# A graph-attention gather loop: the softmax shift from the weights, the running maximum kept ahead of the slope, its parts as upper halves of words

## The chip, the cores and the metric

One core of a Trainium2 chip runs the whole program. The metric is the device time of one execution in microseconds; lower is better.

## What is computed

A GPS layer over 6250 nodes of 256 features and 100000 edges, then a mixture of six experts. `src` is the row (segment) of an edge, `dst` the node that it reads:

```python
# x: [6250, 256], src, dst: [100000]; xn = layernorm(x)
Wh = xn @ W + b
e = (Wh @ a[:256])[dst] + (Wh @ a[256:])[src] + a_b
e = where(e > 0, e, 0.2 * e)
m = segment_max(e, src)                   # one maximum per row
ex = exp(e - m[src])
h = relu(segment_sum(ex / segment_sum(ex, src)[src] * Wh[dst], src))
x = x + h + linear_attention_block(xn)    # with a feed-forward of 1024 and two norms
x = x + experts(layernorm(x))             # 6 experts, top 2
```

## The kernel before

The program is three blocks. The first (to about 754 us) normalises, projects Wh into a table in HBM, computes the linear attention and sorts the edges by rows into tiles of 128. The rows are taken in 50 blocks of 125. The second block (to about 2000 us) is the gather loop. The third is the expert stage.

A row of the table holds 256 values of Wh, the destination term f_dst (column D) and a 1.0 for the denominator: WROW = 258. GpSimd gathers one tile of 128 table rows per indirect DMA (line 1283) into a ring of 44 tiles; SP counts what has landed (`ready`, line 1273) and what has been used (`room`, line 1268).

The other engines work on groups of four tiles that belong to one block, 251 groups. Each engine has a queue written out by hand: `together` takes a list of (lag, stage) and issues, in slot s, each stage for group s - lag. Twenty slots are the body of a loop. In ten slots one pair of row blocks also passes the feed-forward (`feed`: 4 slots of hidden products, 4 of down products on TensorE, the sum and norm on VectorE at slots 0 and 2). One group passes:

- ScalarE fetches its row numbers (`own_rows`, L1459). VectorE adds the shift to the four destination terms of each partition (`shifted`, L1315) and writes for each tile a matrix with that term in the column of the edge's row, zero elsewhere (`mark`, L1322). TensorE turns the four (`turn`, L1565). The terms must be positive for this, which is what the shift is for: one minus the smallest destination term of all nodes, computed after the projection (L688 to L690, L1096, L798 to L802).
- Two slots later VectorE takes the maximum over the group (`group_peak`, L1332), adds the row term (`row_score`, L1338), applies the slope (`row_leaky`, L1343), takes the maximum with the running one (`new_max`, L1350), forms old less new (`old_less_new`, L1357) and keeps it (`keep_max`, L1364). ScalarE makes the turned matrix a 0/1 matrix (`spread`, L1445).
- Three slots after the marks ScalarE splits the new maximum into three bf16 parts (`own_high`, `own_mid`, `own_low`, L1470 to L1483), which stand beside three parts of the row term in `own_all`, computes the factor for old sums (`rescale`, L1489) and distances (`apart`, L1499); TensorE brings row term and maximum to the edges by a product with the 0/1 matrix (`fetch`, L1575).
- Four slots after, VectorE computes the edge's exponent (`score_sum`, `score_edge`, `score_leaky`, `score_less_max`, L1371 to L1388), ScalarE the weight of the last tile (`edge_exp`, L1506) and of the others (`weigh`, L1513), VectorE the last tile's matrix (`own_weight`, L1395).
- Five slots after, TensorE sums weighted rows (`total`, L1586, 8 products) and VectorE adds them to the block's sum (`gather_up`, L1406).

TensorE's queue in a slot is total, fetch, feed-forward products, turn. A helper computes the register address of anything that depends on the group's place or block (L1301, L1308).

## Time and profile before

| | us |
|---|---|
| runs shown | 2505.85, 2507.08, 2512.12; median 2507.08 |
| span of the profiled execution | 2505.8 |
| busy over the span: TensorE, VectorE, ScalarE, GpSimd | 2000.0, 1914.7, 1479.9, 1212.4 |
| gather loop: first gather to last start of line 1406 | 754.4 to 1979.7 |
| third block, 2000 to 2506: TensorE busy | 383.7 |

The profiled execution is 1.3 us under the median. Engines are named PE (TensorE), DVE (VectorE), ACT (ScalarE), POOL (GpSimd), SP; a q behind a name is its instruction queue, where register work stands. In a timeline each row is one instruction (or several merged, xN) with its start, its duration and, in brackets, the idle time of the engine before it and what ended it.

### The profile page before, as it was taken

What the parts mean: (1) busy time and instruction counts of PE and PEld (TensorE: products, weight loads), DVE (VectorE), ACT (ScalarE), POOL (GpSimd) and SP (SyncE); (2) the same over time, 40 slices, a digit from 0 to 9 for tenths busy, and PEclk for the clock granted to TensorE, in tenths of its full rate; (3) what the DMA queues carried; (4) which work ended last, traced back from release to release, by engine and by line L of the source; (5) the groups of instructions that cost most, each with busy time, mean ns of one, the idle gap of its engine ahead of it and who ended that gap; (6) DMA issues with size and microseconds to landing.
All of it is one profiled execution on the core that took longest, in us unless ns stands there. A gap on an engine that the chain in (4) does not pass through costs nothing. (4 is left out here: it accounts for less than half of the span.)

```text
span 2505.8 us, 55059 instructions
## 1 busy us (share of the span) xinstructions
PE 2000.0 (80%) x10267; PEld 1596.8 (64%) x10268; DVE 1914.7 (76%) x6441; ACT 1479.9 (59%) x4950; POOL 1212.4 (48%) x1141
## 2 busy tenths in 40 slices
PE   2888856688855898898888888988989665199997
PEld 1444435577744677677777767767767554188886
DVE  7877689999966898898898898898899763045553
ACT  3566457233304787778788778777878662033332
POOL 0000000011127777777777777777771067455554
PEclk9899967799967899999999989989999866599998
DMA  4200000011113444444444434344440355345553
GB/s 138 54 25 28 25 5 21 13 54 25 21 24 104 119 113 118 114 111 117 113 113 118 110 105 113 111 115 114 117 113 29 92 145 141 86 76 93 94 97 57
DMA packets 125788, 211.73 MB, mean 84 GB/s; under 512 B 35583, under 2 KB 78492, under 8 KB 125476
## 3 DMA queue, kind: packets, MB, share of 16 engines
q0 software_dynamic: 71952, 141.08, 23.7%
q1 hardware_dynamic: 48866, 60.24, 8.2%
q10 hardware_dynamic: 4658, 7.46, 1.0%
q14 instruction: 263, 2.15, 0.3%
q8 instruction: 49, 0.80, 0.1%
HBM read 152.62 MB, written 49.70 MB: 81 GB/s over the span
## 5 line engine op out<-in xcount | busy, mean ns | idle before, releaser
L1283 POOL DMA_INDIRECT area<-wh_table,area x860 | 866.5, 1008 | 284.6 <-issue 257.0
L1586 PE MATMUL bank<-area 128*126 x2008 | 532.7, 412 | 29.4 <-ACT area L1513 20.5
L1586 PEld LDWEIGHTS bank<-area 128*126 128x126 f32 x2008 | 386.2, 203 | 105.0 <-issue 49.5
L1322 DVE TENSOR_SCALAR area<-iota_row,area 128x126 f32<-128x126 f32 x1004 | 343.4, 357 | 0.4 <-issue 0.2
L1499 ACT ACTIVATE area<-iota_row,area 128x126 f32<-128x126 f32 x753 | 269.9, 390 | 0.0
L2077 POOL DMA_INDIRECT out_dram<-area x108 | 169.5, 1569 | 159.3 <-DVE area L2136 142.6
L1513 ACT ACTIVATE area<-area 128x126 f32<-128x126 f32 x753 | 242.4, 385 | 0.0
L515 POOL IOTA acc_mem<- 50x860 f32 x1 | 0.8, 846 | 457.5 <-DVE area L784 457.5
L1606 PE MATMUL bank<-area 128*128 128x250 f32 x800 | 211.4, 410 | 0.0
L1617 PE MATMUL bank<-area 128*125 128x256 f32 x800 | 197.1, 389 | 0.0
L1332 DVE TENSOR_REDUCE area<-bank 125x1 f32<-125x512 f32 x251 | 171.0, 681 | 26.6 <-issue 13.6
L1565 PE MATMUL bank<-ident,area 128*126 128x128 f32 x1004 | 159.5, 283 | 26.7 <-DVE area L1322 26.7
L1445 ACT ACTIVATE area<-bank 125x512 bf16<-125x512 f32 x251 | 144.7, 576 | 59.7 <-DVE area L1332 59.6
L1606 PEld LDWEIGHTS bank<-area 128*128 128x128 f32 x800 | 156.5, 206 | 17.0 <-ACT area L1519 0.2
L1575 PEld LDWEIGHTS bank<-own_all,area 125*128 125x128 bf16 x1004 | 55.0, 99 | 173.7 <-issue 156.5
L1565 PEld LDWEIGHTS bank<-ident,area 128*126 128x126 f32 x1004 | 125.5, 144 | 51.9 <-DVE area L1322 17.4
L2136 DVE SCALAR_TENSOR_TENSOR area<-bank,area 128x256 f32<-128x256 f32 x108 | 47.5, 479 | 145.0 <-DMA out_dram<-area 85.8
L520 POOL DMA_INDIRECT sorted_slots<-area x28 | 46.0, 1641 | 229.3 <-DVE area L855 216.5
L1617 PEld LDWEIGHTS bank<-area 128*125 128x125 f32 x800 | 142.0, 187 | 16.9
L1776 POOL DMA_INDIRECT moe_rows<-area x100 | 120.8, 1208 | 64.7 <-ACT area L1927 35.1
L1575 PE MATMUL bank<-own_all,area 125*128 x1004 | 63.3, 168 | 104.5 <-ACT own_all L1483 84.6
L1406 DVE SCALAR_TENSOR_TENSOR acc_mem<-acc_mem,area,bank 125x258 f32 x251 | 121.2, 483 | 32.2 <-PE bank L1586 24.2
(387 smaller groups left out, 4468.4 us busy)
## 6 DMA issues: line engine op xcount, KB each, us to landing
area<-moe_rows SPq DMA_DIRECT2D x54, 264.0 KB, 2.8
area<-wh_table,area POOLq DMA_INDIRECT x860
area<-area SPq DMA_DIRECT2D x19, 387.0 KB
wh_table<-area SPq DMA_DIRECT2D x50, 126.0 KB
xn<-in_x_dram SPq DMA_DIRECT2D x25, 250.0 KB
x_rows<-area SPq DMA_DIRECT2D x25, 250.0 KB
area<-x_rows ACTq DMA_DIRECT2D x24, 250.0 KB
area<-in_L_ffn_expert_w_dram SPq DMA_DIRECT2D x3, 1536.0 KB, 12.2
```

The costliest lines, as they stand in the source:

```text
L1283: g.indirect_dma_start(out=gath[:, (i + GT) % RS, :], out_offset=None, in_=table, in_offset=bass.IndirectOffsetOnAxis(ap=idx_tab[:, i:i + ...
L1322: ins = V.tensor_scalar(xm[:, b, t, :], iota_row[:, :], rowl[:, j % 10, t:t + 1], fdc[:, b, t:t + 1], ALU.is_equal, ALU.mult)
L1332: V.tensor_reduce(gmax[0:R, b:b + 1], bank[XT[j % 2]][0:R, :], AX.X, ALU.max).then_inc(d_m, 1)
L1406: V.scalar_tensor_tensor(row, row, alpha[0:R, j % 5:j % 5 + 1], bank[US][0:R, 0:WROW], ALU.mult, ALU.add).then_inc(d_acc, 1)
L1445: A.activation(hot[0:R, b, :], bank[XT[j % 2]][0:R, :], ACT.Sign).then_inc(a_hot, 1)
L1499: last = A.activation(dist[:, b, t, :], iota_row[:, :], ACT.Abs, bias=rowl[:, j % 10, t:t + 1], scale=-1.0)
L1513: last = A.activation(sm[:, b, t, :], dist[:, b, t, :], ACT.Exp, bias=e3[:, b, t:t + 1], scale=-1.0e12)
L1565: last = T.transpose(bank[XT[j % 2]][0:RW, t * L:(t + 1) * L], xm[:, b, t, :], ident[:, :])
L1586: last = T.matmul(bank[US][0:RW, 0:WROW], sm[:, b, t, :], gath[:, bass.ds(place + t, 1), :].rearrange("p a w -> p (a w)"), start=(t == 0), ...
L1606: last = T.matmul(bank[HB[p % 2]][:, i * CH:(i + 1) * CH], w_1[:, k, f * 128:(f + 1) * 128], x1T[:, k, :], start=(k == 0), stop=(k == 1))
L1617: last = T.matmul(bank[AB][0:R, r * D:(r + 1) * D], hT[:, f, r * R:(r + 1) * R], w_2[:, f, :], start=(f == 0), stop=(f == 7))
L2077: g.indirect_dma_start(out=out, out_offset=bass.IndirectOffsetOnAxis(ap=rowi[:, j % RB6, s, MW - 2:MW - 1], axis=0), in_=yo[:, j % 3, s, : ...
```

## The change

- A table row has 259 values (TW): column D holds f_dst plus the shift, column D + 1 the 1.0, column D + 2 plain f_dst. `mark` reads column D itself; `shifted` and its buffer are gone. All columns come out of one product with a wider weight matrix, and one addition of a wider bias.
- The shift is 8 times the squared length of the weight vector of f_dst, plus 9, from the weights alone, before the projection (two small products on TensorE at the start). The reduction over nodes and its product are gone.
- The running value `peak` is the maximum of the scores before the slope; the slope is applied to it afterwards. Five VectorE steps on the maximum become two (`row_peak`, `row_leaky`). The old maximum is read from `own_all` by `rescale`, which now computes exp(old - new) itself and stands ahead of the write of the new one.
- `own_all` has fp32 words. A part of a value is the upper half (bf16) of its word, seen through `own_bits`; the next word is the value less that half. On ScalarE the splitting is three steps instead of four.
- The orders of VectorE's and ScalarE's queues change as in the two lists below.
- SP's and VectorE's register values for some waits are bounded by one more register step each.

```diff
+TW = D + 3
...
-        own_all = sb("own_all", [R, NT, 6], BF16)
+        own_all = sb("own_all", [R, NT, 6])
+        own_bits = own_all[:, :, :].rearrange("p b k -> p (b k)").bitcast(BF16).rearrange("p (b k h) -> p b k h", k=6, h=2)[:, :, :, 1]
...
-                    V.tensor_copy(frd[:, t, :], bank[2 + t % 2][0:R, D:D + 2])
-                    V.tensor_tensor(whs[0:R, t % 4, 0:D + 1], bank[2 + t % 2][0:R, 0:D + 1], bias_g[0:R, :], ALU.add).then_inc(p_row, 1)
+                    V.tensor_copy(frd[:, t:t + 1], bank[2 + t % 2][0:R, TW:TW + 1])
+                    V.tensor_tensor(whs[0:R, t % 4, :], bank[2 + t % 2][0:R, 0:TW], bias_g[0:R, :], ALU.add).then_inc(p_row, 1)
...
                 def weights():
...
+                    V.memset(w_a[:, :, D + 1:D + 2], 0.0)
...
-                        for i, vec in enumerate((a_dst, a_src)):
+                        for col, vec in ((D, a_dst), (TW, a_src)):
...
-                                                        accum_out=w_a[:, k, D + i:D + i + 1]))
+                                                        accum_out=w_a[:, k, col:col + 1]))
+                    V.tensor_tensor(wsq, w_a[:, :, D], w_a[:, :, D], ALU.mult).then_inc(w_ready, 1)
+                    V.tensor_copy(w_a[:, :, D + 2], w_a[:, :, D])
...
-                    V.tensor_copy(cdst, bias_g[:, D:D + 1])
+                    V.tensor_copy(bias_g[:, D + 2:D + 3], bias_g[:, D:D + 1])
...
+                    dve.wait_ge(sq_sum, 1)
+                    step(V.tensor_scalar(shift[:, :], bank[2][:, 0:1], 8.0, 9.0, ALU.mult, ALU.add))
+                    step(V.tensor_tensor(bias_g[:, D:D + 1], bias_g[:, D:D + 1], shift[:, :], ALU.add))
...
-                V.tensor_reduce(neg1[0:R, :], frd[:, :, 0], AX.X, ALU.min).then_inc(sh_diag, 1)
-                dve.wait_ge(sh_diag, 2)
-                V.tensor_scalar(fdiag[0:R, 0:R], ident[0:R, 0:R], neg1[0:R, :], None, ALU.mult).then_inc(sh_diag, 1)
...
-                dve.wait_ge(gmap_done, 1)
-                step(V.tensor_reduce(scol, bank[KV][:, 0:R], AX.X, ALU.min))
...
-                step(V.tensor_scalar(scol, scol, cdst, None, ALU.add))
-                step(V.tensor_scalar(shift[:, :], scol, -1.0, 1.0, ALU.mult, ALU.add))
-                step(V.tensor_scalar(fr[:, :], frd[:, :, 1], csrc[0:R, :], None, ALU.add))
-                step(V.tensor_copy(own_all[:, :, 0], fr[:, :]))
-                step(V.tensor_tensor(fr_c[:, :], fr[:, :], own_all[:, :, 0], ALU.subtract))
-                step(V.tensor_copy(own_all[:, :, 1], fr_c[:, :]))
-                step(V.tensor_tensor(own_all[:, :, 2], fr_c[:, :], own_all[:, :, 1], ALU.subtract))
-                V.tensor_scalar(fr_c[:, :], fr[:, :], shift[0:R, :], None, ALU.subtract).then_inc(shift_done, 1)
+                step(V.tensor_scalar(own_all[:, :, 0], frd, csrc[0:R, :], None, ALU.add))
+                step(V.tensor_tensor(own_all[:, :, 1], own_all[:, :, 0], own_bits[:, :, 0], ALU.subtract))
+                V.tensor_tensor(own_all[:, :, 2], own_all[:, :, 1], own_bits[:, :, 1], ALU.subtract)
+                V.tensor_scalar(fr_c[:, :], own_all[:, :, 0], shift[0:R, :], None, ALU.subtract)
...
+                for k in range(2):
+                    last = T.matmul(bank[2][:, 0:1], ones[:, :], wsq[:, k:k + 1], start=(k == 0), stop=(k == 1))
+                last.then_inc(sq_sum, 1)
...
-        gath = take(RS + GT - 1, WROW)
+        gath = take(RS + GT - 1, TW)
...
-        mrun = take(NT)
+        peak = take(NT)
...
+                used = sp.alloc_register("used")
...
-                        sp.reg_load(uses[f % 2], group_tab[32:33, f - RING:f - RING + 1])
+                        sp.reg_load(used, group_tab[32:33, f - RING:f - RING + 1])
+                        sp.reg_alu(uses[f % 2], used, 1, ALU.max)
...
-                V.memset(mrun[0:R, :], -1.0e30)
+                V.memset(peak[0:R, :], -1.0e30)
+                V.memset(own_all[:, :, 3:4], -1.0e30).then_inc(acc_zero, 1)
...
-                def dst_terms(j):
...
-                def shifted(s, j):
...
+                def fetched(j, col):
+                    return gath[:, bass.ds(dve.snap(places[j % 10], min_val=0, max_val=RS - 1), GT), col]
...
                     def stage(s, j):
...
-                        dve.wait_ge(d_x, at(s, 2, 1))
-                        ins = V.tensor_scalar(xm[:, b, t, :], iota_row[:, :], rowl[:, j % 10, t:t + 1], fdc[:, b, t:t + 1],
+                        if t == 0:
+                            dve.wait_ge(a_row, at(s, 1, 1))
+                            wait(dve, p_xt, at(s, 1, -1))
+                        ins = V.tensor_scalar(xm[:, b, t, :], iota_row[:, :], rowl[:, j % 10, t:t + 1], fetched(j, D)[:, t:t + 1],
...
-                def row_score(s, j):
+                def row_peak(s, j):
...
-                    dve.wait_ge(d_m, at(s, 6, 1))
-                    V.tensor_tensor(gt[0:R, b:b + 1], gmax[0:R, b:b + 1], fr_c[:, bass.ds(r, 1)], ALU.add).then_inc(d_m, 1)
+                    dve.wait_ge(d_m, at(s, 3, 1))
+                    V.scalar_tensor_tensor(peak[0:R, bass.ds(r, 1)], gmax[0:R, b:b + 1], fr_c[:, bass.ds(r, 1)], peak[0:R, bass.ds(r, 1)],
+                                           ALU.add, ALU.max).then_inc(d_m, 1)
...
                 def row_leaky(s, j):
...
-                    dve.wait_ge(d_m, at(s, 6, 2))
-                    V.scalar_tensor_tensor(gl[0:R, b:b + 1], gt[0:R, b:b + 1], 0.2, gt[0:R, b:b + 1], ALU.mult, ALU.max).then_inc(d_m, 1)
-                def new_max(s, j):
...
+                    dve.wait_ge(d_m, at(s, 3, 2))
...
-                    V.tensor_tensor(new[0:R, b:b + 1], gl[0:R, b:b + 1], mrun[0:R, bass.ds(r, 1)], ALU.max).then_inc(d_m, 1)
-                def old_less_new(s, j):
...
-                def keep_max(s, j):
...
+                    V.scalar_tensor_tensor(new[0:R, b:b + 1], peak[0:R, bass.ds(r, 1)], 0.2, peak[0:R, bass.ds(r, 1)],
+                                           ALU.mult, ALU.max).then_inc(d_m, 1)
...
                 def score_edge(s, j):
...
-                    V.tensor_tensor(e1[:, b, :], dst_terms(j), pair[:, :, 0], ALU.add).then_inc(d_es, 1)
+                    V.tensor_tensor(e1[:, b, :], fetched(j, D + 2), pair[:, :, 0], ALU.add).then_inc(d_es, 1)
...
                 def score_leaky(s, j):
...
-                                    ALU.is_equal, ALU.mult).then_inc(d_e, 1)
+                                    ALU.is_equal, ALU.min).then_inc(d_e, 1)
...
                 def gather_up(s, j):
...
-                together(dve, [(2, group_peak), (-1, load_place), (4, score_sum), (2, row_score), (0, shifted), (4, score_edge),
-                               (2, row_leaky), (0, mark(0)), (4, score_leaky), (2, new_max), (0, mark(1)), (4, score_less_max),
-                               (0, mark(2)), (2, old_less_new), (0, mark(3)), (2, keep_max), (4, own_weight), (5, gather_up)], feed)
+                together(dve, [(2, group_peak), (-1, load_place), (4, score_sum), (0, mark(0)), (2, row_peak), (4, score_edge),
+                               (0, mark(1)), (2, row_leaky), (4, score_leaky), (0, mark(2)), (4, score_less_max),
+                               (0, mark(3)), (4, own_weight), (5, gather_up)], feed)
...
                 def spread(s, j):
...
-                    act.wait_ge(d_m, at(s, 6, 1))
+                    act.wait_ge(d_m, at(s, 3, 1))
...
-                def own_part(s, j, k):
+                def own_word(j, k):
...
-                def own_high(s, j):
-                    act.wait_ge(d_m, at(s, 6, 4))
+                def own_high(j, k):
+                    r = act.snap(blocks[j % 5], min_val=0, max_val=NT - 1)
+                    return own_bits[:, bass.ds(r, 1), 3 + k:4 + k].rearrange("p a k -> p (a k)")
+                def rescale(s, j):
+                    b = j % 2
+                    act.wait_ge(d_m, at(s, 3, 3))
+                    wait(act, d_acc, at(s, 1, -4))
+                    A.activation(alpha[0:R, j % 5:j % 5 + 1], new[0:R, b:b + 1], ACT.Exp, bias=own_word(j, 0), scale=-1.0).then_inc(a_alpha, 1)
+                def own_first(s, j):
...
-                    A.copy(own_part(s, j, 0), new[0:R, j % 2:j % 2 + 1]).then_inc(a_own, 1)
-                def own_mid(s, j):
+                    act.wait_ge(a_alpha, at(s, 1, 1))
+                    A.copy(own_word(j, 0), new[0:R, j % 2:j % 2 + 1]).then_inc(a_own, 1)
+                def own_second(s, j):
...
-                    A.activation(own_part(s, j, 1), own_part(s, j, 0), ACT.Identity, bias=new[0:R, b:b + 1], scale=-1.0)
-                    A.activation(left[0:R, b:b + 1], own_part(s, j, 0), ACT.Identity, bias=new[0:R, b:b + 1], scale=-1.0).then_inc(a_own, 1)
-                def own_low(s, j):
...
+                    A.activation(own_word(j, 1), own_high(j, 0), ACT.Identity, bias=new[0:R, b:b + 1], scale=-1.0).then_inc(a_own, 1)
+                def own_third(s, j):
...
-                    A.activation(own_part(s, j, 2), own_part(s, j, 1), ACT.Identity, bias=left[0:R, b:b + 1], scale=-1.0).then_inc(a_own, 1)
-                def rescale(s, j):
-                    b = j % 2
-                    act.wait_ge(d_m, at(s, 6, 5))
-                    wait(act, d_acc, at(s, 1, -4))
-                    A.activation(alpha[0:R, j % 5:j % 5 + 1], gd[0:R, b:b + 1], ACT.Exp).then_inc(a_alpha, 1)
+                    A.activation(own_word(j, 2), own_high(j, 1), ACT.Identity, bias=own_word(j, 1), scale=-1.0).then_inc(a_own, 1)
...
                     def stage(s, j):
...
-                        act.wait_ge(d_x, at(s, 2, 2))
+                        act.wait_ge(d_x, at(s, 1, 1))
...
-                together(act, roots, [(3, own_high), (3, apart([0])), (3, own_mid), (2, spread), (3, own_low), (4, edge_exp), (3, apart([1, 2])), (3, rescale),
-                                       (4, weigh), (-1, own_rows)], feed)
+                together(act, roots, [(3, rescale), (3, apart([0])), (3, own_first), (2, spread), (3, own_second), (4, edge_exp), (3, apart([1])), (3, own_third),
+                                       (3, apart([2])), (4, weigh), (-1, own_rows)], feed)
...
                 def turn(s, j):
...
-                    pe.wait_ge(d_x, at(s, 2, 2))
+                    pe.wait_ge(d_x, at(s, 1, 1))
...
-                        last = T.matmul(bank[QE][:, 6 * t:6 * t + 6], hot[0:R, b, t * L:(t + 1) * L], own_all[:, bass.ds(r, 1), :].rearrange("p a k -> p (a k)"),
+                        last = T.matmul(bank[QE][:, 6 * t:6 * t + 6], hot[0:R, b, t * L:(t + 1) * L], own_bits[:, bass.ds(r, 1), :].rearrange("p a k -> p (a k)"),
...
-                        last = T.matmul(bank[US][0:RW, 0:WROW], sm[:, b, t, :], gath[:, bass.ds(place + t, 1), :].rearrange("p a w -> p (a w)"),
+                        last = T.matmul(bank[US][0:RW, 0:WROW], sm[:, b, t, :], gath[:, bass.ds(place + t, 1), 0:WROW].rearrange("p a w -> p (a w)"),
```

## Rows read from the trace of the kernel before

**Rows 1.** Windows: stretch, its us; PE, PEld, DVE, ACT, POOL busy; clock, DMA share, GB/s

```profile
1200.00:1500.00 300.00, 261.66 (x1410) 210.51 (x1409) 267.00 (x1131) 236.10 (x941) 226.34 (x226) 0.93 0.41 113
```

**Rows 2.** GpSimd's gathers: source view of line 1283 with idle causes; its timeline

```profile
L1283 POOL DMA_INDIRECT area<-wh_table,area x860: 992/998/1473, 754.4 to 1891.1; - x172
...
  SPq L1268: 14.2, 16
...
1891.11 1.00 POOL L1283 DMA_INDIRECT area<-wh_table,area  x1 [0.31 <-issue]
```

**Rows 3.** Timeline of VectorE: start us, us, line, operation, count, idle before with its releaser

```profile
1496.50 0.48 DVE L1406 SCALAR_TENSOR_TENSOR acc_mem<-acc_mem,area,bank 125x258 f32 x1 [0.83 <-PE bank L1586]
...
1499.44 0.68 DVE L1332 TENSOR_REDUCE area<-bank 125x1 f32<-125x512 f32 x1
...
1502.94 0.48 DVE L1406 SCALAR_TENSOR_TENSOR acc_mem<-acc_mem,area,bank 125x258 f32 x1
...
1523.07 0.48 DVE L1406 SCALAR_TENSOR_TENSOR acc_mem<-acc_mem,area,bank 125x258 f32 x1
...
1524.07 0.17 DVE L1371 TENSOR_REDUCE area<-bank 128x8 f32<-128x24 f32 x1
...
1527.16 0.48 DVE L1406 SCALAR_TENSOR_TENSOR acc_mem<-acc_mem,area,bank 125x258 f32 x1 [0.19 <-PE bank L1586]
```

**Rows 4.** Waits between 850 and 1850 us (total, times, longest); ScalarE's timeline

```profile
ACT area L1459 <- SPq L1273: 6.9, 6, 2.1
...
1909.70 0.28 ACT L1459 ACTIVATE area<-area,iota_blk 128x4 f32 x1
```

**Rows 5.** Timeline of VectorE, the small steps of one slot

```profile
1520.12 0.18 DVE L1371 TENSOR_REDUCE area<-bank 128x8 f32<-128x24 f32 x1
1520.34 0.16 DVE L1338 TENSOR_TENSOR area<-area,fr_c 125x1 f32<-125x1 f32 x1
1520.59 0.23 DVE L1315 TENSOR_SCALAR area<-area,shift 128x4 f32 x1
1520.85 0.17 DVE L1377 TENSOR_TENSOR area<-area 128x4 f32<-128x4 f32 x1
1520.96 0.16 DVE L1343 SCALAR_TENSOR_TENSOR area<-area 125x1 f32<-125x1 f32 x1
1521.07 0.35 DVE L1322 TENSOR_SCALAR area<-iota_row,area 128x126 f32<-128x126 f32 x1
1521.33 0.16 DVE L1382 SCALAR_TENSOR_TENSOR area<-area 128x4 f32<-128x4 f32 x1
1521.50 0.16 DVE L1350 TENSOR_TENSOR area<-area 125x1 f32<-125x1 f32 x1
1521.58 0.34 DVE L1322 TENSOR_SCALAR area<-iota_row,area 128x126 f32<-128x126 f32 x1
1521.84 0.15 DVE L1388 TENSOR_TENSOR area<-area 128x4 f32<-128x4 f32 x1
```

**Rows 6.** Timeline of TensorE, two fetches (line 1575)

```profile
1522.68 0.25 PE L1575 MATMUL bank<-own_all,area 125*128 x4
...
1555.58 0.25 PE L1575 MATMUL bank<-own_all,area 125*128 x4 [0.45 <-ACT own_all L1483]
```

**Rows 7.** Register work in VectorE's queue for line 1308: min/median/max ns

```profile
L1308 DVEq FUSED_REGOPS  x378: 92/93/93, 900.4 to 1799.0; - x189
```

**Rows 8.** Timeline of ScalarE

```profile
1522.02 0.20 ACT L1506 ACTIVATE area<-area 128x1 f32<-128x1 f32 x1 [0.52 <-DVE area L1388]
1522.13 0.67 ACT L1499 ACTIVATE area<-iota_row,area 128x126 f32<-128x126 f32 x2
1522.71 0.19 ACT L1489 ACTIVATE area<-area 125x1 f32<-125x1 f32 x1
...
1555.04 0.29 ACT L1483 ACTIVATE own_all<-own_all,area  x1
```

**Rows 9.** Source view of line 798

```profile
L798 DVE TENSOR_REDUCE acc_mem<-bank x1: 286/286/286, 468.1 to 468.1; 128x1 f32<-128x125 f32 x1
```

More of the change, by code:

```diff
@@ L51 @@
 LAG = 5
-SPARE = 820
+SPARE = 940
 SLOT, TAB_SLOTS = 6, 8
@@ L216, in gps_kernel @@
         xr = take(2, D)
-        w_a = take(2, WROW)
+        w_a = take(2, D + 4)
         w_kv = take(2, 2 * D)
-        bias_g = take(D + 1)
+        bias_g = take(TW)
         bias_k, bias_v = take(D), take(D)
@@ L226, in gps_kernel @@
         vaug = take(2, 2, R + 4)
-        whs = take(4, WROW)
+        whs = take(4, TW)
         scratch = take(D)
-        fdiag = take(128)
+        wsq = take(2)
         tri, trin = take(128), take(128)
@@ L245, in gps_kernel @@
         more = take(128)
-        fr, rstd_all, nmr = (take(NT)[0:R] for _ in range(3))
-        mvs, frd = take(NT, 2)[0:R], take(NT, 2)[0:R]
+        rstd_all, nmr = (take(NT)[0:R] for _ in range(2))
+        mvs, frd = take(NT, 2)[0:R], take(NT)[0:R]
         ti = wbase.rearrange("p k b -> p (k b)").bitcast(I32)
@@ L318, in gps_kernel @@
         int50 = smallt[6].bitcast(I32)
-        gcol, scol, neg1, cdst, csrc, tcol, wcol, tq0, tq1 = (take(1) for _ in range(9))
+        gcol, csrc, tcol, wcol, tq0, tq1 = (take(1) for _ in range(6))
         srci, dsti = wpos.bitcast(I32), bpos.bitcast(I32)
@@ L1062, in products @@
                     for k in range(2):
-                        last = T.matmul(bank[2 + j][0:R, 0:WROW], xT[:, j, k, :], w_a[:, k, :], start=(k == 0), stop=(k == 1))
+                        last = T.matmul(bank[2 + j][0:R, 0:D + 4], xT[:, j, k, :], w_a[:, k, :], start=(k == 0), stop=(k == 1))
                     last.then_inc(p_wk, 1)
@@ L2087, in _ @@
                 clears = [dve.alloc_register(f"clear{i}") for i in range(4)]
+                found = [dve.alloc_register(f"found{i}") for i in range(2)]
                 def expert(j):
```

55 lines of the change are left out of this document (17 added, 38 removed).

## The prediction

> **What bounds the kernel now.** I read the windows first. In the gather loop (754 to 1980 us, 251 groups) no engine stands out: of 300 us TensorE is busy 262, VectorE 267, ScalarE 236, GpSimd 226 [rows 1]. So busy time doesn't name the bound. Three views after it do.
>
> GpSimd's own stream: 860 gathers from 754.4 on, 1.00 us each with 0.30 between, the last at 1891.1, and 14.2 us of waiting for a free place in the ring [rows 2]. 0.3 us of each of those 16 waits is the usual gap, so some 9.4 us are real, and gathering alone would end near 1882.7.
>
> The consumer's slots, from one start of line 1406 to the next: 6.4 us (1496.50 to 1502.94) and 4.09 (1523.07 to 1527.16) [rows 3]. In every ten slots, three are long (VectorE has the norm work of the feed-forward in its queue in two of them), seven are 3.9 to 4.2. The 241st fetch of row numbers (line 1459) is the first that needs the last gathered tile. It runs at 1909.7 without a wait [rows 4], some 15.7 us after the last gather has had about 2 us to land. So the consumer is behind at the end, and what it gains or loses is seen, except early: between 850 and 1106 it still waited 6.9 us for gathered rows [rows 4], and a slower consumer would wait less there.
>
> What paces a slot. VectorE's small steps and marks follow each other at 0.08 to 0.26 us with no hole [rows 5], and added up over a slot without a wait they are some 3.9 us. TensorE's own slot is 4.09: its fetch at 1522.68 leads to the line 1406 at 1527.16, 4.48 us and one slot later, and no TensorE row there shows a wait [rows 3, 6]. Both are near 4 us, so the order of the small steps between engines matters more than their number.
>
> **The change part by part.** VectorE, per slot: out go lines 1315, 1338, 1343, 1350, 1357, 1364; in come row_peak and row_leaky. I price a step by the distance to the next start. Out: 0.26 + 0.25 + 0.11 + 0.08 + 0.08 (line 1357, as 1350) + 0.10 (line 1364, nearly as 1343) = 0.88 [rows 5]. In: 0.26 and 0.11, 0.37. Each mark now reads its scalar at a computed place, and that computation stands in VectorE's queue: 93 ns each [rows 7]. Behind a mark (0.26 to the next start) it is hidden, behind a small step not: lines 1338 to 1315 and 1315 to 1377, which have it, are 0.25 and 0.26 apart, 1343 to 1322 without it 0.11. Marks 1 to 3 stand behind small steps now at 0.11, 0.17 and 0.08. I take 0.16 to 0.25, together 0.12 to 0.39 more, by the middle 0.26. Saved: 0.88 - 0.37 - 0.26 = 0.25 us per slot; bounds 0.51 (addresses hidden) and 0.05 (mark 0 and the two new steps pay too).
>
> But score_less_max, on which ScalarE's edge_exp waits, does not come sooner. Now it starts 1.72 us after line 1371 (1520.12 to 1521.84). It moves from behind mark 1 to behind mark 2: 0.22 to mark 0, 0.26, 0.26, 0.20 to mark 1, 0.26, 0.11, 0.20 to mark 2, 0.26 = 1.77; with hidden addresses 1.44. I take 1.72, unchanged.
>
> ScalarE: one step less, but own_third, the last part of the maximum, is moved past edge_exp and one apart; before, own_low stood ahead of both. A mover pays its queue: own_third is ready at edge_exp + 0.11 + 0.29 + 0.29 = + 0.69 us [rows 8]. TensorE's fetch waits for it, and behind that fetch stand in TensorE's queue the feed-forward products, the turn and the next total. From the end of line 1483 (1555.04 + 0.29) to the fetch that waited for it (1555.58) is 0.25 us [rows 6, 8].
>
> That closes a ring that now is open: line 1406 + 1.00 (1523.07 to line 1371 at 1524.07 [rows 3]) + 1.72 (to 1388) + 0.18 (1521.84 to edge_exp, 1522.02) + 0.69 + 0.25 = fetch at + 3.84 us. Without a wait it starts 3.70 after it: 0.39 ahead of the next line 1406 (1522.68, 1523.07), and a slot is 4.09 [rows 3, 6]. From the fetch 4.48 us to the line 1406 of the slot after: 8.32 us for two slots, 4.16 each, against 4.09. At the bounds 1.44 and 1.90 for the step from 1371 the ring is 8.04 (below TensorE's own 8.18: nothing lost) and 8.50.
>
> Slot 3, behind the norm work, pays more. Now VectorE's line 1332 at 1499.44 leads to the seventh line 1406 after it at 1527.16, 27.7 us [rows 3]. In between TensorE fetches early, ahead of edge_exp. With the ring: 0.60 (line 1332 to 1371, of the 1.00) + 1.72 + 0.18 + 0.69 + 0.25 + 4.48 = 7.92 to the second line 1406; the next follows after TensorE's 4.09 (12.0), and from there two rounds of 8.32: 28.65. That is 0.9 us more per ten slots. In slots 0 to 2 VectorE is the pace: 0.25 less once or twice, of which TensorE's total takes a part, since line 1406 waited 0.83 us for it at 1496.50 already [rows 3]: some -0.4 in the ten behind the loop's jump, 0 in the other, -0.2 on average. Together +0.7 us per ten slots, in 24.6 tens 17.2 us, less some 4.5 in the first six tens, where waits for gathered rows hide it: 12.7 us.
>
> Other parts. TensorE reads the parts with a step of two, 6 columns in products of 0.25 us for four: nothing. The gather's rows have 1036 bytes for 1032: GpSimd's 1.00 us [rows 2] and a DMA share of 0.41 [rows 1] leave that at nothing. Odd word starts of xm, sm and gathered rows: no row shows a price; tiles at several starts take the same 0.34 [rows 5], so nothing, at most 0.1 per slot. Before the loop the reduction (0.29 us, line 798 [rows 9]) and four steps of about 0.2 go from VectorE's chain, and some five steps with a round trip to TensorE come into weights(): between -1.3 and +1 us, zero. Register steps in SP and in the last stage stand where the engine waits: nothing, at most 5 us (54 tiles, 0.1 each).
>
> Sum: 2505.8 + 12.7 = 2518.5 for the profiled execution, which is 1.3 below the median of the runs shown: 2519.8, say **2520**.
>
> **The rivals.**
> 1. It saves time: the ring stays open, because addresses are computed behind marks and score_less_max comes 0.28 sooner. Then VectorE's 0.51 counts in slots 0, 1 and 3 of ten, less what TensorE's total eats: 0.4 to 0.8 us per ten, 10 to 20 us; the gathering holds it at 15.7 + 9.4 = 25. 2487 to 2498. For it: VectorE runs those slots without a hole. Against it: 0.25 against 0.11 at computed places. If a removed step were worth its whole duration, the saving would be 0.23 + 3 x 0.16 + 2 x 0.15 less 2 x 0.16 = 0.69 per slot and the 25 us would be reached, 2482. Line 1322 takes 0.34 while the next starts after 0.26, so durations overlap [rows 5]. The Trainium skill, "VectorE: DVE Perf Modes", section "The DRAIN you can't avoid", says that the next operation doesn't start until the pipeline is empty, but that one which isn't held starts earlier; the trace agrees with the second half, and the first would give this 2482.
> 2. Nothing: the ring costs 0 to 0.3 per ten slots and what VectorE saves pays for it, the rest turns to wait before line 1406. 2500 to 2512.
> 3. Slower still: every mark and new step pays its addresses in full, 1.90 for 1.72. Slot 3 comes 0.18 later and each of two rounds: +1.2 per ten, 30 us less 5: 2530 to 2535.
> The forecast decides at one point: own_third's end against the end of TensorE's total. If it comes 0.14 us sooner than worked out, the ring is open and rival 1 or 2 holds.
>
> **How the numbers follow.** Forecast (2511 to 2532) 0.45, rival 1 0.22, rival 2 0.27, rival 3 0.06. Beyond 2532: 0.07; below 2490: 0.11. Range 2490 to 2532. Under 0.3% (7.5 us) a change can't be told from none here. Slower than 2514.6: 0.40 of the forecast's and rival 3, 0.46. Faster than 2499.6: 0.22. Same: 0.32.
>
> **What would show it.** Right: TensorE's fetch waits for ScalarE's own_third in most slots, in slot 3 by about a microsecond; quick slots 4.1 to 4.2; twenty slots near 97.1 us for 95.7; GpSimd waits longer for the ring; the loop ends near 1992. Rival 1: twenty slots under 95, those waits gone in the quick slots, ScalarE waiting for gathered rows beyond 1106. Rival 2: twenty slots 95.3 to 96.2. Rival 3: VectorE's distances from small step to mark at 0.25 or more. Wrong altogether: another time before 754 or after the loop, which I take as fixed.

## The result and the profile after

| | before | after |
|---|---|---|
| median, us | 2509.6 (4 runs, 2505.9 to 2512.6) | 2565.6 (4 runs, 2560.1 to 2579.8) |
| profiled span, us | 2505.8 | 2560.4 |
| first gather, us | 754.4 | 747.6 |
| last start of gather_up (before line 1406, after line 1385) | 1979.7 | 2032.3 |
| VectorE: busy us, instructions | 1914.7, 6441 | 1816.6, 5437 |

The ratio is 1.0243, 95% interval 1.0222 to 1.0263: 56 us slower, where 10 slower was forecast. The spans split the 54.6 us between them so: the gather begins 6.8 us sooner, from there to the last gather_up the loop takes 1284.7 us for 1225.3 (+59.4), and what follows takes 528.1 for 526.1.

The gathers (this view answers [rows 2]) and some of the waits (us in total, times, longest) between 850 and 1850 us, all of after:

```profile
L1283 POOL DMA_INDIRECT area<-wh_table,area x860: 992/998/1518, 747.6 to 1934.1; - x172
...
  SPq L1268: 68.0, 41
```

```profile
DVE acc_mem L1385 <- PE bank L1568: 139.4, 150, 2.5
PE bank L1557 <- ACT own_all L1471: 127.6, 82, 3.6
```

And the rows of before that answer to these two waits:

```profile
PE bank L1575 <- ACT own_all L1483: 70.5, 60, 2.9
...
DVE acc_mem L1406 <- PE bank L1586: 14.2, 30, 1.0
```

VectorE's busy time fell by 98 us as meant, and gather_up waits for TensorE's total 125 us more in this one millisecond. TensorE in turn waits for own_third, in 82 of its 199 fetches of that millisecond. GpSimd's gathers cost what they did (998 ns), but wait 68 us for room: they are held by the consumer.

Where the loop's time went is seen slot by slot. This table is worked out from the starts of gather_up in the two traces: the mean length of each of the twenty slots of a loop body, over the 61st to 240th of the 251 slots (column 8 and 18 are the slot behind VectorE's norm work, called slot 3 in the prediction).

```
column      0    1    2    3    4    5    6    7    8    9   10   11   12   13   14   15   16   17   18   19    sum
before   3.95 4.27 3.95 4.08 4.12 6.53 4.72 6.48 3.91 4.24 3.89 3.98 4.18 4.07 6.72 6.89 4.49 6.50 4.17 3.91  95.06
after    4.43 4.19 4.38 4.09 4.51 5.99 5.65 5.82 6.06 4.17 4.45 4.13 4.15 4.12 6.52 6.23 5.06 5.76 5.87 4.24  99.82
```

Columns 8 and 18 lose 3.85 us together; the eleven quick ones (0 to 4, 9 to 13, 19) 2.22; 6 and 16 1.50; the five in which VectorE is the pace (5, 7, 14, 15, 17) win 2.80. That is 4.77 per twenty, and 12.5 twenties make the 59.4 us. Where VectorE is the pace a sooner gather_up shortens its own slot and lengthens the one behind, so the slots around the norm are best read together: columns 5 to 8 and 14 to 18 take 50.4 us before and 52.9 after, 2.5 more.

**A quick slot of after.** Rows of VectorE, ScalarE and TensorE, in order of time, some left out:

```profile
1503.28 0.48 DVE L1385 SCALAR_TENSOR_TENSOR acc_mem<-acc_mem,area,bank 125x258 f32 x1 [1.05 <-PE bank L1568]
...
1504.43 0.18 DVE L1350 TENSOR_REDUCE area<-bank 128x8 f32<-128x24 f32 x1
...
1506.07 0.16 DVE L1367 TENSOR_TENSOR area<-area 128x4 f32<-128x4 f32 x1
...
1506.26 0.20 ACT L1488 ACTIVATE area<-area 128x1 f32<-128x1 f32 x1 [1.09 <-DVE area L1367]
1506.37 0.39 ACT L1481 ACTIVATE area<-iota_row,area 128x126 f32<-128x126 f32 x1
1506.82 0.29 ACT L1471 ACTIVATE own_all<-own_all  x1
...
1507.37 0.25 PE L1557 MATMUL bank<-own_all,area 125*128 x4 [0.22 <-ACT own_all L1471]
...
1511.85 0.48 DVE L1385 SCALAR_TENSOR_TENSOR acc_mem<-acc_mem,area,bank 125x258 f32 x1 [1.03 <-PE bank L1568]
```

This is the ring of the prediction, closed: gather_up + 1.15 (score_sum, line 1350) + 1.64 (score_less_max) + 0.19 (edge_exp) + 0.56 + 0.29 (own_third starts and ends) + 0.26 = fetch at + 4.09, and 4.48 from there to the gather_up of the slot after: 8.57 for two slots.

**Slot 3 of after**, twice: once with TensorE's clock down, once not.

```profile
1526.66 0.69 DVE L1328 TENSOR_REDUCE area<-bank 125x1 f32<-125x512 f32 x1
...
1529.40 0.48 DVE L1385 SCALAR_TENSOR_TENSOR acc_mem<-acc_mem,area,bank 125x258 f32 x1
1529.40 0.29 ACT L1471 ACTIVATE own_all<-own_all  x1
...
1529.95 0.25 PE L1557 MATMUL bank<-own_all,area 125*128 x4 [1.91 <-ACT own_all L1471]
1530.06 2.54 PE L1588 MATMUL bank<-area 128*128 128x250 f32 x8
...
1532.39 1.06 PE L1547 MATMUL bank<-ident,area 128*126 128x128 f32 x4
...
1533.24 2.61 PE L1568 MATMUL bank<-area 128*126 x8
...
1536.07 0.48 DVE L1385 SCALAR_TENSOR_TENSOR acc_mem<-acc_mem,area,bank 125x258 f32 x1 [2.27 <-PE bank L1568]
```

```profile
1632.03 0.25 PE L1557 MATMUL bank<-own_all,area 125*128 x4 [1.85 <-ACT own_all L1471]
1632.14 1.94 PE L1588 MATMUL bank<-area 128*128 128x250 f32 x8
1633.91 0.60 PE L1547 MATMUL bank<-ident,area 128*126 128x128 f32 x4
1634.35 1.91 PE L1568 MATMUL bank<-area 128*126 x8
...
1636.48 0.48 DVE L1385 SCALAR_TENSOR_TENSOR acc_mem<-acc_mem,area,bank 125x258 f32 x1 [0.38 <-PE bank L1568]
```

The windows of the first (columns as in [rows 1]; the third number from the end is the granted clock, 1.00 is 2.4 GHz and 0.50 is 1.2):

```profile
1528.00:1530.00 2.00, 0.09 (x3) 0.06 (x3) 1.99 (x9) 1.26 (x6) 1.70 (x2) 1.00 0.41 102
1530.00:1532.00 2.00, 2.00 (x12) 1.74 (x13) 1.35 (x6) 2.00 (x8) 1.39 (x3) 0.81 0.31 97
1532.00:1534.00 2.00, 2.00 (x8) 1.72 (x7) 1.38 (x7) 1.71 (x8) 1.70 (x2) 0.50 0.47 112
```

Both times the fetch waits 1.9 us for own_third with TensorE idle. The second time the clock stays up and the slot is 5.00; the first time it falls to 0.50 (1.2 GHz) behind the idle time, the three pieces up to the next total take 6.21 for 4.45 us, and the slot is 6.67. Of the 24 slots of this kind in the loop 9 are 4.9 to 5.0, with a granted clock of 1.00 throughout; 14 are 6.4 to 6.7 and one is 8.0, with a mean clock of 0.58 to 0.74. In the kernel before they are 3.6 to 4.3, all of them, at 1.00. What decides between the two after nearly the same idle time isn't shown.

### The profile page after: what moved, and what is told of

Same layout as the page of the kernel before. It is cut to its first block and busy times, and to the rows that moved or that the text cites. A ratio compares the mean times of both kernels' runs of the same rounds, so it can differ in the third digit from the quotient of the medians.

```text
span 2560.4 us, 52267 instructions
## 1 busy us (share of the span) xinstructions
PE 2020.1 (79%) x10269; PEld 1610.6 (63%) x10270; DVE 1816.6 (71%) x5437; ACT 1489.0 (58%) x4699; POOL 1216.0 (47%) x1137
## 5 line engine op out<-in xcount | busy, mean ns | idle before, releaser
L1568 PEld LDWEIGHTS bank<-area 128*126 128x126 f32 x2008 | 393.5, 207 | 86.5 <-issue 28.8
L1318 DVE TENSOR_SCALAR area<-iota_row,area 128x126 f32<-128x126 f32 x1004 | 355.6, 365 | 61.0 <-ACT area L1438 48.4
L1481 ACT ACTIVATE area<-iota_row,area 128x126 f32<-128x126 f32 x753 | 290.7, 386 | 0.0
L1588 PE MATMUL bank<-area 128*128 128x250 f32 x800 | 220.9, 424 | 0.1
L1557 PEld LDWEIGHTS bank<-own_all,area 125*128 125x128 bf16 x1004 | 48.3, 99 | 253.3 <-issue 244.7
L1547 PE MATMUL bank<-ident,area 128*126 128x128 f32 x1004 | 164.8, 291 | 11.0 <-DVE area L1318 10.9
L1547 PEld LDWEIGHTS bank<-ident,area 128*126 128x126 f32 x1004 | 132.3, 149 | 34.5 <-DVE area L1318 11.8
```

What stands on the lines that cost most here:

```text
L1318: ins = V.tensor_scalar(xm[:, b, t, :], iota_row[:, :], rowl[:, j % 10, t:t + 1], fetched(j, D)[:, t:t + 1], ALU.is_equal, ALU.mult)
L1481: last = A.activation(dist[:, b, t, :], iota_row[:, :], ACT.Abs, bias=rowl[:, j % 10, t:t + 1], scale=-1.0)
L1547: last = T.transpose(bank[XT[j % 2]][0:RW, t * L:(t + 1) * L], xm[:, b, t, :], ident[:, :])
L1568: last = T.matmul(bank[US][0:RW, 0:WROW], sm[:, b, t, :], gath[:, bass.ds(place + t, 1), 0:WROW].rearrange("p a w -> p (a w)"), start=(t = ...
L1588: last = T.matmul(bank[HB[p % 2]][:, i * CH:(i + 1) * CH], w_1[:, k, f * 128:(f + 1) * 128], x1T[:, k, :], start=(k == 0), stop=(k == 1))
```

## The experiments

One thing has to be known to read their times. On most chips and occasions of the experiments every kernel, the one before too, took 2847 to 2924 us, since the sequencers of several engines stopped again and again while the gather ran (the last section shows it). There whole times hardly tell the orders apart, so those runs are read in the last nineteen slots, behind the last gather. They are 82.7 us in the kernel before (one trace) and 86.9 and 86.2 in the changed one (two). Single slots mostly repeat within 0.1 us between the traces of one kernel, but where TensorE's clock falls in one trace and not in another a sum can differ by up to 1.9 us, and a difference of less than that says little by itself. Two occasions gave 2506 for the kernel before, and the two runs made there carry the most.

**1. own_third ahead of edge_exp.** Two pairs of neighbours change places with it, own_first with distance 0 and own_second with spread; all else is as changed:

```
- (3, apart([0])), (3, own_first), (2, spread), (3, own_second), (4, edge_exp), (3, apart([1])), (3, own_third),
-  (3, apart([2])), (4, weigh), ...
+ (3, own_first), (3, apart([0])), (3, own_second), (2, spread), (3, own_third), (4, edge_exp), (3, apart([1])),
+  (3, apart([2])), (4, weigh), ...
```

> The changed kernel, with one order undone: on ScalarE own_third stands ahead of edge_exp again (rescale, own_first, mark distance 0, own_second, spread, own_third, edge_exp, the two other distances), as own_low did before. Theory A (the loss is the ring: difference of scores on VectorE, edge_exp, one distance, own_third, TensorE's fetch): the fetch no longer waits for own_third in the quick slots, twenty slots fall from 99.8 to 94 to 95.5 us, and the time is 2485 to 2505, the gather starting 7 us sooner than before included. Theory B (the loss lies in the marks that read at computed places, in mark 0 that waits for ScalarE's own_rows, or in rows of 1036 bytes): the order of ScalarE's small steps gives back less than 15 us, 2550 or more. Theory C (both, half and half): 2520 to 2535.

> The changed kernel with own_third ahead of edge_exp, once more, beside the changed kernel itself. Theory A: 0.97 to 0.985 of the changed kernel where the kernel before takes 2510 (2485 to 2515), the loop's twenty slots 94 to 96. Theory B: over 0.99 of it.

> The changed kernel with own_third ahead of edge_exp, on another chip, since the first two chips of the experiments ran the kernel before at 2900 us, with stops of 1 to 3 us between the sequencers' register steps on every engine. Where the kernel before takes 2510, theory A (ring) expects 2485 to 2515 and no wait of the fetch for own_third in the quick slots; theory B (marks, rows) 2550 or more. On a chip of 2900, both expect 0.99 to 1.00 of the kernel before.

On the first chip 2876.8 for 2904.0 (0.9926, 0.9894 to 0.9959), on the second 0.9934. On the third, where the kernel before takes 2506.4: 2512.4, ratio 1.0026 (1.0009 to 1.0044). So this one order gives back about 50 of the 56 us, set against the kernel before on each occasion: twenty slots 95.7 (the first expectation had 94 to 95.5), columns 8 and 18 4.47 and 4.28, no slot of that kind over 4.5 and the granted clock 1.00 in all of them. What it gives back lies around the norm: columns 5 to 8 and 14 to 18 take 48.9 us for 52.9, the eleven quick ones 46.8 for 46.9. And it isn't faster than before, though VectorE has 1000 instructions less. A quick slot of it in which ScalarE also has feed-forward work (two steps, from 1276.79 to 1277.59, stand ahead of these rows), ScalarE's row by row:

```profile
1277.49 0.29 ACT L1454 ACTIVATE area<-area,own_all 125x1 f32<-125x1 f32 x1
1277.97 0.19 ACT L1460 COPY own_all<-area 125x1 f32 x1 [0.19 <-ACT area L1454]
1278.08 0.40 ACT L1481 ACTIVATE area<-iota_row,area 128x126 f32<-128x126 f32 x1
1278.41 0.29 ACT L1466 ACTIVATE own_all<-own_all,area  x1
1278.61 0.58 ACT L1424 ACTIVATE area<-bank 125x512 bf16<-125x512 f32 x1
1279.14 0.29 ACT L1471 ACTIVATE own_all<-own_all  x1
1279.34 0.18 ACT L1488 ACTIVATE area<-area 128x1 f32<-128x1 f32 x1
...
1279.56 0.35 DVE L1374 TENSOR_SCALAR area<-iota_row,area 128x126 f32<-128x126 f32 x1 [0.69 <-ACT area L1488]
...
1279.68 0.25 PE L1557 MATMUL bank<-own_all,area 125*128 x4
```

Here the fetch doesn't wait (it still does in the slots around the norm, 0.8 to 1.0 us in the slot behind it). VectorE's own_weight (line 1374) waits 0.69 us for edge_exp instead, and ScalarE has no hole but the 0.19 that own_first waits for rescale. Its list, from one slot to the next, is 4.28 us, over TensorE's 4.09: in such slots ScalarE is the pace. So this run settles the slots around the norm; what the place of own_third costs in quick slots is seen only in part 6, where ScalarE's holes are filled.

**2. The same move in the kernel before**: own_low behind edge_exp and one distance, nothing else but the bounds of two registers.

```
- (3, own_mid), (2, spread), (3, own_low), (4, edge_exp), (3, apart([1, 2])), (3, rescale),
+ (3, own_mid), (2, spread), (4, edge_exp), (3, apart([1])), (3, own_low), (3, apart([2])), (3, rescale),
```

> The kernel before, with one order changed alone: ScalarE's own_low (the last part of the maximum) moved from ahead of edge_exp to behind edge_exp and one distance, where the changed kernel has own_third. Two registers on which engines wait are bounded as in the change; nothing else. Theory A (ring): this alone makes the loss of the loop, twenty slots 95.1 to 98.5 to 100.5 us, 2545 to 2570. My own forecast's size for the same ring (4.16 for 4.09 in quick slots, 0.9 more in slot 3) would be 2518 to 2525. Theory B: own_low has slack there, 2506 to 2514.

> The kernel before with own_low behind edge_exp and one distance, once more. Theory A: the loss of the change's loop from this order alone, ratio to the kernel before 1.015 to 1.025 where that takes 2510; the size of the forecast would be 1.004 to 1.006. Theory B: 1.000 to 1.002.

> The kernel before with own_low behind edge_exp and one distance, on a chip where the kernel before takes 2505 to 2510 if it is one. The changed kernel with its order undone took 2512 for 2565, so the place of the last part is worth some 50 us there. Theory A, the ring alone (edge_exp, one distance, the last part, the fetch) makes it, whatever the rest of the list is: then the kernel before loses 35 to 55 us by the same move, 2545 to 2565. Rival D, the ring costs so much only together with the other edits of the change (rescale at the head of ScalarE's list, mark 0 ahead of row_peak and waiting for own_rows): 2510 to 2530, about the size of my forecast.

> The kernel before with own_low behind edge_exp and one distance. In the slots behind the last gather it already showed 4.25, 4.42, 4.32 for 4.26, 3.88, 3.99 and 5.82 for 3.61 behind the norm: 3.1 us more in thirteen slots, 4.6 us in nineteen. If the place alone makes the loss, the whole time is 2550 to 2570 where the kernel before takes 2507 (4.5 more in each twenty slots, twelve and a half twenties); if it needs the change's other edits, 2510 to 2530. On a chip of 2880 to 2900: 1.00 to 1.01 whatever the cause.

> The kernel before with own_low late, on another chip. If the place alone makes the loss: 2550 to 2570 where the kernel before takes 2507, every slot behind the norm's second half at 5.0 or 5.8 for 3.9. If not: 2510 to 2530. On a chip of 2880 to 2900: 1.00 to 1.01.

> The kernel before with own_low late, on one more chip. If the place alone makes the loss: 2550 to 2570 where the kernel before takes 2507. If it needs the change's other edits: 2510 to 2530. On a chip of 2880 to 2900: 1.00 to 1.01 of the kernel before, as three times already.

It ran six times, each time at 2898 to 2924 for 2884 to 2905: ratios 1.0028 to 1.0112, where the changed kernel itself has 0.9936 (below). Its whole time where the loop isn't disturbed was never measured, and the 2550 to 2570 expected stay untested. The last nineteen slots are plain: 87.2 us in four runs and 88.9 in two, for 82.7. The slot behind the norm there, first with own_low late (the sixth run), then in the kernel before:

```profile
2316.14 0.68 DVE L1334 TENSOR_REDUCE area<-bank 125x1 f32<-125x512 f32 x1
...
2318.38 0.20 ACT L1508 ACTIVATE area<-area 128x1 f32<-128x1 f32 x1 [0.92 <-DVE area L1390]
...
2318.78 0.28 ACT L1485 ACTIVATE own_all<-own_all,area  x1
...
2319.27 0.25 PE L1577 MATMUL bank<-own_all,area 125*128 x4 [2.12 <-ACT own_all L1485]
2319.38 3.59 PE L1608 MATMUL bank<-area 128*128 128x250 f32 x8
...
2325.39 0.48 DVE L1408 SCALAR_TENSOR_TENSOR acc_mem<-acc_mem,area,bank 125x258 f32 x1 [2.25 <-PE bank L1588]
```

```profile
1927.18 0.68 DVE L1332 TENSOR_REDUCE area<-bank 125x1 f32<-125x512 f32 x1
...
1928.39 0.29 ACT L1483 ACTIVATE own_all<-own_all,area  x1
1928.90 0.25 PE L1575 MATMUL bank<-own_all,area 125*128 x4
...
1929.42 0.20 ACT L1506 ACTIVATE area<-area 128x1 f32<-128x1 f32 x1 [0.74 <-DVE area L1388]
1930.56 0.48 DVE L1406 SCALAR_TENSOR_TENSOR acc_mem<-acc_mem,area,bank 125x258 f32 x1
```

In the kernel before, own_low is done before edge_exp's input is there, and the fetch comes 1.72 us behind line 1332. Moved behind edge_exp it comes 3.13 behind it, TensorE idles 2.12, its clock falls (granted 0.62, then 0.52, in the next two stretches of 2 us; the products of the feed-forward take 3.59 for the 1.94 of other slots), and the slot is 5.87 for 3.61. It is 5.8 to 5.9 in all six runs. The place alone, in the old kernel and with none of the change's other edits, makes both parts of the loss in this slot, the idle time and the clock, and 4.5 us or more in the last nineteen slots, where the change loses 3.5 to 4.2. That it makes the whole loop's 59 us is a conclusion from this and the first experiment, not a measurement.

**3. The changed kernel again, beside the others.**

> The changed kernel itself, unaltered, beside the orders of the next three runs on one chip. On a chip where the kernel before takes 2510: 2555 to 2575. On a chip on which all engines stop in the loop for reasons of their own (the kernel before at 2900), theory A (the ring of small steps is what costs) expects the loss to be of the size of the single order in the run of the kernel before with own_low late, a ratio of 1.00 to 1.015; theory B (marks and rows) 1.02 or more.

2884.9 for 2904.9, ratio 0.9936 (0.9913 to 0.9958); last nineteen slots 86.2. The same kernel with own_third early took 2888.8 beside it (0.9934): where something else stops the loop, the change's later order costs nothing that shows in the whole time, and it comes out ahead. Both theories had expected it slower than the kernel before, and both were wrong.

**4. The difference of scores sooner on VectorE**, ScalarE as changed:

```
- (0, mark(1)), (2, row_leaky), (4, score_leaky), (0, mark(2)), (4, score_less_max),
- (0, mark(3)), ...
+ (2, row_leaky), (4, score_leaky), (0, mark(1)), (4, score_less_max), (0, mark(2)),
+ (0, mark(3)), ...
```

> The changed kernel, ScalarE's order as changed, but on VectorE the difference of scores (score_less_max) stands ahead of mark 2, row_leaky and score_leaky ahead of mark 1, so it starts some 0.3 to 0.4 us sooner after score_sum. Theory A (ring): the ring of two quick slots falls from 8.57 to 8.2, the bound of TensorE's own 8.18; slot 3 comes 0.4 to 0.8 us sooner too: twenty slots 96 to 97 us for 99.8, 2510 to 2530. Theory B (cost of computed places, own_rows, odd rows): every step is still there, 2555 to 2570.

> The changed kernel with the difference of scores ahead of mark 2, once more, beside the changed kernel itself. Theory A: the ring falls from 8.57 to 8.2 per two quick slots, 2510 to 2535 where the kernel before takes 2510. Theory B: no gain, 2555 or more. A third result, a gain as large as with own_third early, would say that the ring sits at its edge and that either piece opens it.

0.9939 and 0.9912 on two occasions of 2900. In the last slots it helps where it should, but little: behind the norm 4.82 in both runs (4.90 and 6.58 in the two of the changed kernel), the next four 4.31, 4.06, 4.10, 4.10 for 4.32, 4.06, 4.27, 4.09, and nineteen slots 85.5 to 85.7 us. That is about 1 of the 4 us that the changed kernel loses there; the 2510 to 2530 of theory A weren't tested. The edit moves the difference less than expected, 0.15 us (in the slot that is 4.10 in both kernels it starts 1.49 behind score_sum for 1.64, where 0.3 to 0.4 was expected), and the two slots that the ring spans there fall by as much: 4.10 and 4.37 for 4.10 and 4.51. Done together with the first edit it adds next to nothing (84.9 for 85.0 to 86.9), since ScalarE is the pace there:

> Both orders of the two runs before this one at once: own_third ahead of edge_exp on ScalarE, the difference of scores ahead of mark 2 on VectorE. Theory A: with own_third early the ring is already open, so the second order adds only what edge_exp itself holds: 0 to 8 us less than the first alone, 2480 to 2505. Theory B: 2545 or more, as with each alone.

**5. own_third next behind edge_exp**, alone, and with row_peak and the difference of scores sooner on VectorE:

> The changed kernel, own_third next behind edge_exp, ahead of both distances, nothing else: a smaller dose of the same cause. Behind edge_exp it starts 0.20 later for 0.55, so the ring of two quick slots falls from 8.57 to 8.2, and slot 3 has it 0.35 sooner. Theory A (the loss goes with the lateness of own_third): 2515 to 2535 where the kernel before takes 2507. If the position behind edge_exp as such is what costs (own_third is made late by the difference of scores whatever stands between): 2550 or more. In the last nineteen slots: 84.5 to 86 under A, 86.5 or more under the other.

> A version meant to beat both kernels: the changed kernel with own_third next behind edge_exp (ahead of both distances) and on VectorE row_peak ahead of mark 0, score_leaky ahead of mark 1, the difference of scores ahead of mark 2. The ring as the traces measure it: line of gather_up + 1.00 + 1.43 (1.79 less the mark and the gap) + 0.19 + 0.50 (third next: 0.20 + 0.29) + 0.26 = fetch at + 3.38, ahead of the 3.70 at which TensorE comes to it; ScalarE's own slot some 4.1. Theory A (ring) expects quick slots of 4.09 to 4.2, the slot behind the norm 3.9 to 4.3 and TensorE's full clock in it, twenty slots 93 to 95, and 2480 to 2500 where the kernel before takes 2507. Theory E (ScalarE's list is the next bound, as with own_third ahead of edge_exp, 4.28): 2505 to 2515. On a chip of 2880 to 2900 only the last slots, behind the last gather, can be compared: 81 to 83 us for the last nineteen under A (the kernel before 82.7, the changed one 86.9), 84.5 to 85.5 under E.

88.3 and 87.4 us for nineteen slots, most quick slots 4.3 to 4.5: the first lies where the rival of theory A had it (86.5 or more), the second above both theories (0.9948 and 0.9966 of the kernel before, on one occasion of 2900). The rows of the second show why:

```profile
2318.76 0.19 ACT L1488 ACTIVATE area<-area 128x1 f32<-128x1 f32 x1
...
2319.29 0.29 ACT L1471 ACTIVATE own_all<-own_all  x1 [0.34 <-issue]
```

Behind the short edge_exp own_third starts only 0.53 us later, 0.34 of it with no work on the engine: it has three operands at computed places, and the register steps for them (lines 1442 and 1471, from 2318.89 to 2319.23 in ScalarE's queue) begin only behind the issue of edge_exp, whose 0.2 us don't hide them. Nothing is won against one distance between them (0.56), and both distances and weigh stand behind the hole. With it ScalarE's list is 4.33 us from slot to slot, so ScalarE is the pace here too.

**6. own_third early and every gap filled:**

```
+ (3, rescale), (3, apart([0])), (3, own_first), (3, apart([1])), (3, own_second), (2, spread), (3, own_third),
+  (4, edge_exp), (3, apart([2])), (4, weigh), ...
```

> The changed kernel with own_third ahead of edge_exp and each step of the chain on ScalarE followed by work that doesn't depend on it: rescale, distance 0, own_first, distance 1, own_second, spread, own_third, edge_exp, distance 2. With own_third early but rescale and own_first back to back ScalarE's list took 4.28 us per slot, 0.2 to 0.3 of it a wait of own_first for rescale and a repeated gap. Theory E (ScalarE's own list was what was left): the list falls to 4.0, below TensorE's 4.09; quick slots 4.09, twenty slots 93 to 94.5 for 95.7, 2480 to 2497 where the kernel before takes 2507, last nineteen slots 81 to 83 us. Its rival: what was left came from mark 0 waiting for own_rows and from computed places on VectorE, then the slots stay at 4.2 to 4.3 and the time at 2505 to 2515, last nineteen slots 84.5 to 85.5.

> The version with the gaps on ScalarE filled, on another chip. Theory E: 2480 to 2497 where the kernel before takes 2507, twenty slots 93 to 94.5; its last slots on the first chip were 4.09 to 4.14 where they had been 4.28. On a chip of 2880 to 2900: 0.985 to 0.993 of the kernel before.

> The version with the gaps on ScalarE filled, on one more chip. By its last slots (61.8 us for fourteen of which the kernel before makes 61.3) the loop takes as long as that of the kernel before, and the set-up 7 us less: 2495 to 2508 where the kernel before takes 2507. My first expectation for it, 2480 to 2497, holds if the stretches where VectorE is the pace gain more than these last slots show. On a chip of 2880 to 2900: 0.983 to 0.992 of the kernel before.

0.9892 and 0.9864 on two occasions of 2900; where the kernel before takes 2505.8: **2493.0, ratio 0.9939 (0.9916 to 0.9962)**. It is 0.6% faster than the kernel before. Twenty slots are 93.9 us, the quick ones 4.06 to 4.28, columns 8 and 18 4.2; the eleven quick ones together 45.4 for 46.9 in the changed kernel and 44.6 before, the columns around the norm 48.5 for 52.9 and 50.4. ScalarE's list in the slots with feed-forward work is 4.0 to 4.1 us, holes left out. The first expectation (2480 to 2497) holds; the second, from the last slots alone, began 2 us too high. Its waits between 850 and 1850 us, and the gathers' wait for room:

```profile
DVE acc_mem L1385 <- PE bank L1568: 59.2, 95, 1.5
...
ACT area L1438 <- SPq L1273: 14.4, 9, 4.7
```

```profile
L1283 POOL DMA_INDIRECT area<-wh_table,area x860: 994/999/1491, 750.9 to 1880.2; - x172
...
  SPq L1268: 4.6, 14
```

The gathers wait for room no more, and ScalarE waits for gathered rows again: the gathering is close behind as the next bound.

## Why the prediction was wrong

- **The direction and the mechanism were right.** The ring closes as forecast; the fetch waits for own_third; GpSimd waits for room. Rivals 1 and 2 are out, and rival 3's cost isn't there in the ring shown (1.64 us for its 1.90). But the wait is not in most slots, as the signs had it: 82 of 199 fetches between 850 and 1850 us (60 of 209 before), since in a ring of two slots only one fetch waits. The deciding point (own_third against the end of TensorE's total) was the right one; only it was read as a matter of 0.14 us in quick slots.
- **The step that failed: the 4.48 us from the fetch to the next gather_up in slot 3.** The time to the fetch was right, even a little long (line 1328 to the fetch 3.29 us, forecast 0.60 + 1.72 + 0.18 + 0.69 + 0.25 = 3.44). From the fetch, 4.48 was added, a value of slots in which TensorE doesn't idle; with the clock up it is 4.45, but in 15 of 24 slots the clock fell and in the one shown it was 6.12. I forecast a wait of about a microsecond there (it was 1.9) and gave it no consequence. At some 1.65 us each, that is 25 of the 47 us by which the loop lost more than forecast. The Trainium skill, "TensorE: Matmul & The Clock Gate", section "A second HAM failure mode: psum-queue depth-cycling", says that repeated short idle times between groups of matmuls can make the clock go back and forth. The trace of after agrees in 15 of the 24 slots, and the kernel before already showed such a fall in the slot after the one in which TensorE idles through the norm:

```profile
1490.57 0.25 PE L1575 MATMUL bank<-own_all,area 125*128 x4 [2.61 <-ACT own_all L1483]
...
1492.48 3.80 PE L1586 MATMUL bank<-area 128*126 x8 [0.56 <-ACT area L1513]
```

  The eight products take 3.80 for 1.91 us, at a granted clock of 0.50. Slot 3 should have been priced at both levels.
- **Quick slots: 8.57 for 8.32.** By terms: gather_up to score_sum 1.15 for 1.00, score_sum to the difference 1.64 for 1.72, edge_exp to the end of own_third 0.85 for 0.69 (the step behind a distance starts 0.45 later, not 0.29: computed places again), the rest as forecast. The excess over TensorE's 8.18 was sized 0.14 and is 0.39. Over the loop the eleven quick columns lost 28 us, where the sum had some 7 (two rounds per ten slots at 0.14).
- **The gain of VectorE** was sized 0.2 us per ten slots where it is the pace. In the changed kernel it can't be told from the loss in the slots behind; with own_third early columns 5 to 8 and 14 to 18 take 1.5 us less than before, in twenty slots. Right in kind, and sized too small.
- **The 4.5 us hidden early** by waits for gathered rows were not hidden. From the ninth gather_up to the fifty-ninth the changed kernel lost 2.6 us per ten slots, as much as later.
- **Rescale ahead of own_first** I didn't price at all. It costs nothing while ScalarE has slack; with own_third early, the wait of own_first for it is part of the next bound (4.28).
- **Before the loop** zero was forecast. In this execution the gather starts 6.8 us sooner; over all traces it starts at 748.8 on average with the new set-up (13) and 752.5 with the old (7), so about 4 is the change's, with single traces from 742 to 753. The after-loop part, forecast at nothing up to 5, is 2.0.
- Marks that read at computed places, odd word starts and rows of 1036 bytes: the gathers still take 998 ns, and with own_third early and the gaps filled the loop is faster than that of the kernel before, so together they cost less than the removed steps gave. They were not measured one by one. Mark 0 waits for own_rows (up to 0.7 us); that this costs anything wasn't separated either.

## What to carry over

Before moving a step to a later place in an engine's list, ask who waits for it and what that engine is doing meanwhile: a wait that makes TensorE idle for 2 us costs the idle time and then, in more than half of the cases here, most of that again in clock. Removing instructions from an engine pays only where its order keeps the others fed: the same set of removed steps was worth + 56 us or - 13 us by the order of ScalarE's list alone. And look whether a short step hides the computed operands of the next: here one of 0.2 us didn't (0.34 us idle), one of 0.39 did all but 0.06.

## What the runs showed of the hardware

In 16 of the 18 runs the kernel before took 15 to 16% longer than the 2507 us known of it, and every other kernel about as much. It isn't the chip alone: one and the same chip ran the kernel before at 2506 and, later, at 2887 us. The set-up is as quick (first gather at 750.0 us in the run shown below) and so are the slots behind the last gather; only while the gathers run do the sequencers stop. The changed kernel: VectorE's register work of the line that loads the places (min, median, max ns) in the first run, then in such a run:

```profile
L1247 DVEq FUSED_REGOPS  x220: 57/65/65, 854.0 to 1953.8; - x110
```

```profile
L1247 DVEq FUSED_REGOPS  x220: 15/65/730, 904.7 to 2254.7; - x110
```

The median is the same, but single steps of 65 ns take up to 730 here. Over the sixteen such traces register steps of VectorE and ScalarE take up to 1.4 us and those of SP up to 1.0, all steps over 0.3 us lying between the first gather and 1.2 us behind the start of the last; those of TensorE's queue never take over 0.12 us. In the four other traces no step on any engine takes over 0.18. What stops them isn't shown. The Trainium skill, "Advanced Engine Details and Errata", section "ISA Cache", gives the instruction cache two lines of 256 instructions each (more on TensorE). A body of twenty slots has 766 recorded instructions on VectorE and 796 on ScalarE, so by an estimate from these counts and that size it would be fetched anew each time round beside the gathers' transfers. That TensorE's steps are spared would fit, but no run here tests it. A comparison made on such an occasion can have another sign: the changed kernel is 1.024 of the kernel before on one and 0.994 on the other.
